# One signal a unit in place of two for TensorE's transposes and products in a graph network's dense stages

## The reference

```
x = layernorm(x + L0(x))   # 2 SAGE convolutions: mean of neighbours @ W_l + b + x @ W_r, rows divided by their norm, relu
x = layernorm(x + L1(x))   # 4 SAGE convolutions without the norm: relu(mean @ W_l + x @ W_r + b)
x = layernorm(x + L2(x))   # attention with 4 heads over the edges, + x @ W1.T + b1, relu, normalised
x = layernorm(x + L3(x))   # transformer convolution over the edges, + x @ Wskip.T + b, relu, batch norm over all nodes
```

## Time and profile before

| what | value |
|---|---|
| median of 3 runs | 16911.43 us (16896.66 to 16914.56) |
| profiled execution | the page gives its span alone: 16848.3 us from the first to the last instruction |
| busy: PE, DVE, ACT, POOL | 8724.5, 7447.1, 4895.5, 7480.4 us |
| mean granted TensorE clock | 0.667 |
| tables of edges, before round 0 | to about 1729 us |
| rounds 0 to 7 end at about | 3350, 5390, 6860, 8340, 9800, 11470, 13860, 16226 us |

### The profile page before, as it was taken

The page is one execution under the profiler, slowest core; times in us unless marked ns, Lnnn a source line. Parts: engine busy times, 40 slices in busy tenths (PEclk is TensorE's granted clock), DMA queues, the critical chain, the costliest instruction groups (busy, mean ns, idle before and its releaser), DMA issues. The chain is left out here.

```text
span 16848.3 us, 221135 instructions
## 1 busy us (share of the span) xinstructions
PE 8724.5 (52%) x38799; PEld 6051.7 (36%) x38898; DVE 7447.1 (44%) x21114; ACT 4895.5 (29%) x11500; POOL 7480.4 (44%) x7460
## 2 busy tenths in 40 slices
PE   6654344533344455445545544454544446677765
PEld 2121233422333344334434433343333323344444
DVE  6654234424454122121112113447888864444456
ACT  0000122223444122122212213344555541222257
POOL 2545554354322654554465455433334336554410
PEclk9775566756666566566656766666666667777776
DMA  6000234424443245345424534554333331233367
GB/s 253 1 3 1 75 120 139 156 71 125 135 143 121 87 148 171 94 126 159 152 88 148 171 97 143 169 190 147 120 121 119 120 113 47 79 98 110 118 193 245
DMA packets 1169327, 2072.17 MB, mean 123 GB/s; under 512 B 283810, under 2 KB 292531, under 8 KB 1156371
## 3 DMA queue, kind: packets, MB, share of 16 engines
q1 hardware_dynamic: 662400, 1128.29, 22.2%
q10 hardware_dynamic: 268534, 564.37, 8.7%
q0 software_dynamic: 238336, 378.92, 8.3%
HBM read 1358.91 MB, written 773.68 MB: 127 GB/s over the span
## 5 line engine op out<-in xcount | busy, mean ns | idle before, releaser
L639 POOL DMA_INDIRECT agg<-y_rows,s_idx x3136 | 3246.2, 1035 | 5507.4 <-ACT y_rows L970 2718.8
L883 PE MATMUL o_bank<-b_parts,ones_parts 3*128 3x512 bf16 (+1 forms) x1568 | 786.2, 501 | 3838.8 <-ACT h_t L1043 2893.0
L886 PE MATMUL o_bank<-w_r,h_t 128*128 128x128 f32 x12544 | 2587.7, 370 | 0.0
L1594 DVE TENSOR_TENSOR total<-o_bank,agg_in 128x512 f32<-128x512 f32 (+1 forms) x1568 | 1048.1, 688 | 3377.2 <-DMA agg_in<-agg 2068.9
L886 PEld LDWEIGHTS o_bank<-w_r,h_t 128*128 128x128 f32 x12544 | 2204.2, 264 | 536.9 <-issue 536.2
L1043 ACT ACTIVATE h_t<-ht_bank 128x512 f32<-128x512 f32 (+1 forms) x1568 | 878.3, 594 | 3930.8 <-remote 2694.1
L883 PEld LDWEIGHTS o_bank<-b_parts,ones_parts 3*128 3x128 bf16 (+1 forms) x1568 | 148.9, 95 | 4192.2 <-ACT h_t L1043 3123.9
L970 ACT ACTIVATE y_rows<-edge_bank,inv 128x128 f32<-128x128 f32 x2352 | 658.7, 373 | 2807.7 <-remote 1640.9
L789 PE MATMUL edge_bank<-w_l,run 128*128 128x128 f32 x4704 | 962.0, 383 | 951.7 <-DVE run L1410 776.4
L630 POOL DMA_INDIRECT gath<-node_a,g_idx x1176 | 1124.9, 957 | 513.6 <-issue 355.1
L630 POOL DMA_INDIRECT gath<-node_x,g_idx x784 | 780.1, 995 | 1079.4 <-PE edge_bank L829 646.1
(11 more groups left out here) (257 smaller groups left out, 14785.5 us busy)
## 6 DMA issues: line engine op xcount, KB each, us to landing
agg_in<-agg SPq DMA_DIRECT2D x1560, 256.0 KB
node_a<-h_out ACTq DMA_DIRECT2D x780, 256.0 KB
h_in<-node_a SPq DMA_DIRECT2D x780, 256.0 KB
node_x<-h_out ACTq DMA_DIRECT2D x392, 256.0 KB
node_b<-h_out ACTq DMA_DIRECT2D x392, 256.0 KB
h_in<-node_x SPq DMA_DIRECT2D x390, 256.0 KB
h_in<-node_b SPq DMA_DIRECT2D x390, 256.0 KB
agg<-zeros ACTq DMA_DIRECT2D x96, 1024.0 KB
```

The source lines that it names most:

```text
L639: pool.indirect_dma_start(agg[order(r)], bass.IndirectOffsetOnAxis(s_idx[q][:, k:k + 1], 0), y_rows[q][:, k, :], None, bounds_check=N - 1, ...
L883: pe.matmul(o_bank[s][0:p, :], ones_parts[:, 0:p], b_parts[:, r, :].unsqueeze(1).to_broadcast([3, RPP, P]), start=True, stop=False, skip_g ...
L886: last = pe.matmul(o_bank[s][0:p, j * P:(j + 1) * P], h_t[s][:, j, 0:p], w_r[r][:], start=False, stop=j == RPP - 1, skip_group_check=True)
L1594: dve.tensor_tensor(flat(total[s], p), o_bank[s][0:p, :], flat(agg_in[s], p), ALU.add).then_inc(sum_ready[s], 1)
```

## The change

`htp_ready` and `mm_ready` become stages with one semaphore for both row groups. PE raises each only after the second group (`if s == 1`), in the eight rounds and in the last stage. All who waited for the semaphore of group s, for either group, now wait for the one semaphore. What is computed and its order on every engine stay.

```
-        htp_ready = unit_stage("htp_ready", all_store)
+        htp_ready = both_stage("htp_ready", all_store)
-        mm_ready = unit_stage("mm_ready", all_store)
+        mm_ready = both_stage("mm_ready", all_store)
...
                     for s in range(2):
-                        sp.wait_ge(htp_ready[s], htp_ready.at(r, u))
+                        sp.wait_ge(htp_ready[0], htp_ready.at(r, u))
                         sp.sem_inc(sp_turn, 1)
                         sp.dma_start(flat(h_in[s], width(u, s)), group_dram(h_of, u, s)).then_inc(h_loaded[s], 16)
...
                             last = pe.transpose(ht_bank[s][:, j * P:j * P + p], h_in[s][0:p, j, :], ident[0:p, 0:p])
-                        last.then_inc(htp_ready[s], 1)
+                        if s == 1:
+                            last.then_inc(htp_ready[0], 1)
...
                                              start=False, stop=j == RPP - 1, skip_group_check=True)
-                        last.then_inc(mm_ready[s], 1)
+                        if s == 1:
+                            last.then_inc(mm_ready[0], 1)
...
-                        act.wait_ge(htp_ready[s], htp_ready.at(r, u + 1))
-                        act.wait_ge(mm_ready[s], mm_ready.at(r, u))
+                        act.wait_ge(htp_ready[0], htp_ready.at(r, u + 1))
+                        act.wait_ge(mm_ready[0], mm_ready.at(r, u))
...
-                        dve.wait_ge(mm_ready[s], mm_ready.at(r, u + 1))
+                        dve.wait_ge(mm_ready[0], mm_ready.at(r, u + 1))
```

## The result

The changed kernel took 16976.29 us (median of 4 runs, 16964.83 to 16999.09) against 16904.04 us (4 runs, 16877.71 to 16914.56) of the kernel before: a ratio of 1.0047, 95% interval 1.0033 to 1.0061. It is **0.5% slower**, where 1.5% faster was forecast. The profiled execution after has a span of 16997.1 us, 148.8 us over that of before, about twice the difference of the medians (72 us), so single stages are to be read with some tens of us of play.

The account below looks back on a forecast made before the run. With no engine busy over 52%, order and waiting were taken to set the time, with PE's signals late during POOL's indirect DMAs. -82 - 83 - 119 - 52 + 75 = -261 us from 16911 gave 16650 us; 8-in-10 range 16350 to 17100.

Parts of the forecast that it names:

- If the signals pass one by one: Sage rounds 2 to 4, POOL's stretches: fewer PE signals let copies come earlier; 19 pairs at 4.3 us, -82 us.
- -119: First sage round: copies and squares move earlier, 5 us for 16 pairs and 3 us for 13 longer ones.
- -52: Sixth sage round: the same gain as in the first, 26 pairs at 2 us each.
- the single signals are delayed as long as four were: Sage rounds, POOL's stretches: the named sign by which the forecast of 16650 us would fail.
- Held in its queue by the reload of h: Longer pairs, rounds 2 to 4: SP's agg load waits behind h's reload; an earlier signal saves 49 x 1.7, 83 us.
- rival B: Signals aren't dear, or the DMAs' end rules; longer pairs keep their length: 16911 within 34 us, or 16950 to 16985; chance 0.20.
- +75 for the coarser signal: Sage rounds outside POOL's stretches: first copy waits for four more transposes, 349 copies at 0.43 us, half taken.
- So I take 0: Transformer round: DVE's sum must clear the same bank before products, hiding the wait; uncovered, 42 or 84 us by clock.
- Attention, 0: Attention round: DVE sets the pace and hides the coarser signal's delay; otherwise 42 us would show.
- Last stage, 0 and at worst +42: Last stage: ACT is the pacer, so the coarser signal costs 0, at worst 42 us.
- Rival A: POOL's stretches: the single signal comes at the later group's hour, so group 0's products move back; 17090 to 17165 us; chance 0.16.
- The prediction's sum by that rule, 16940 us: Whole kernel: at 26.3 ns each, 1764 fewer increments gain at most 46 us, against +75 us for coarser waits.

Follow-up runs that it names:

- before, again: The kernel before, unchanged, profiled again on another chip than that of the first profile: 13983.48 us, ratio 0.9991 to the kernel before.

## Why the prediction was wrong

The sum was -82 - 83 - 119 - 52 + 75 = -261 us; the medians say +72, the profiles +149. All five terms stand for the sage rounds (the other stages were put at 0); these were to get 261 us shorter and took 129 us more.

**"If the signals pass one by one" (-82, and the base of -119 and -52): the step that failed.** It lets the single signal take an earlier place because fewer signals go ahead of it. The profile after has half the signals, on the same chip, and they are as late as before. I counted the units of the sage rounds whose transposes end within 18 us of the pair's first scatter and whose second copy comes over 3 us after them, from the starts and ends of PE's and ACT's instructions. Before there are 199; the first copy comes 10.3 us after its group's transposes, the second 12.9. After there are 197, and either copy comes some 12.5 us after its group's transposes. So the common signal has the lateness of the second group's, and the first group's copy loses 2 us. In the first round 13 units had late copies more than 1.5 us apart before, in the sixth 12: in all 25 the first copy after stands nearer to the place of the second one before than to that of the first, counted from the pair's first scatter.

Pair for pair, counted by the starts of POOL's first scatters, the 19 of rounds 2 to 4 that were to save 82 us are 8 us shorter together. Four became 25.5 us long, the gain that was forecast; four, among them the very pair of the earlier trace rows, grew by 2.4 to 3.0 us, with their copies at 22.3 to 23.1 us, where the second one had been; the others lie between. The 29 pairs of the first round that were to save 119 us are 30 us longer, the 26 of the sixth that were to save 52 are 9 us longer. The signs that were named for the forecast say the same: ACT's unnamed waits rose, POOL's wait for `y_rows` rose, and "the single signals are delayed as long as four were".

That PE's signals are what is late, and not ACT, is right: the trace's semaphore events have `htp_ready[0]` raised at 6111.18 and `htp_ready[1]` at 6116.12, some 12 and 17 us after the transposes of the earlier trace rows. What the lateness counts in is open. It is not the number of these signals alone, as the profile after shows. Nor are PE's signals alone slow: in rounds 2 to 4, over 6 us into a stretch, SP's add instructions that wait for nothing take 0.69 us (median of 120), and in "before, again" never more than 0.04. When the stretch of the earlier trace rows is over, the four signals of PE that are due are all raised within 0.22 us (7971.82 to 7972.04).

**"Held in its queue by the reload of h" (-83): failed.** It was a misreading of the rows before: SP had issued both reloads by 7965.36 (7961.11 + 4.25), 6.4 us ahead of the load of `agg` at 7971.72. In between stand only SP's own small instructions, four of them 0.7 us long. After, both reloads are issued by 8041.5, and the load still comes at 8047.16, some 2.7 us after POOL's last DMA, as before. The 49 longer pairs of rounds 2 to 4 are 13 us longer together and not 83 shorter. That the end of the stretch rules was rival B's reason against the term.

**+75 for the coarser signal: right in kind.** On the chips without late signals it can be seen alone: +98 us in the sage rounds, half by ACT's wait and half by SP's. SP's I had put at 0 ("a load has several us to land").

**"So I take 0" for the transformer round: failed**, +76 us on the first chip, +94 on the others. The cover named there, DVE's sum in the same bank, ended PE's wait in 40 of the 98 units before and in 3 with ACT's wait for both. The bound without cover, 42 us at the high level of the clock and 84 at the low one, holds the first chip's +76, but it counted the wait and not what goes with it in clock: ACT's wait alone cost 107 us, 83 of them in PE's busy time.

**Attention, 0: right** (+7 and 0). DVE is busy for 1977 us of it; that this is why was not tested. **The products' coarser signal** had a part in the +75 (the first sum waits for one more group of products, 1.2 to 2.4 us). On the other chips it cost nothing that shows in any stage; on the first it was not run alone.

**Last stage, 0 and at worst +42: wrong in sign**, -71 us. SP's wait for both groups makes this gain, and ACT's wait for its store goes with it. Why the queue is the quicker for it is not shown.

**The rivals.** Rival A's mark, both copies at the hour of the second, is there in the pair that it was argued from, and in 21 of the 25 units of the first and sixth rounds counted above (within 1 us of the second copy's place in the stretch); in rounds 2 to 4 the single signal comes anywhere between the two hours and beyond. Its price, 181 us or more, was too high: the sage rounds took 129 us more here, and 98 us more on the chips where no signal is late, so what is left for it is some 30 us, within the play of one profile. Rival B's mark, longer pairs that keep their length, is there as well. The time is that of B in its slower form, 16950 to 16985 us, but partly by luck: the sage rounds alone took more than its 75 us, and the transformer round's loss and the last stage's gain, both left out, nearly cancel.

## What to carry to other kernels

Before a wait that is late is counted as gain, follow the pair to its end and ask what else is released at the same hour: here SP's load came with the end of POOL's DMAs whatever PE signalled. Fewer signals are no gain until it is shown that their number is what they wait for. A merged signal delays the first half by the second half's work; in a round that PE paces, four fifths of its price was not the idle time that it added but PE's own work at a lower granted clock (83 of 107 us). Merge signals for each waiter and each stage on its own: the same edit lost 94 us in one stage and gained 67 us in another, by another engine's wait.

## What was not expected of the hardware

The same kernel takes 16904 us on one chip and 13996 to 14008 us on three others. Stages in which POOL issues most take the difference (rounds 2 to 4: 1467 to 1480 us against 1134 to 1137), attention and last stage none (2373 and 2363, 621 and 619). On the slower one ACT's copies follow PE's transposes by 12 and 17 us while POOL issues indirect DMAs; in "before, again" by 0.7 us. Counted as above, 199 units have late copies in the slower chip's profile and 29 to 33 in those of the other chips. On the slower one SP's add instructions are slow as well within the stretches (0.69 us, median, for 0.03). Why isn't known; it may be the chip or something around it.

On a chip without late signals more completion signals cost nothing: 12 more in each of 588 units, between -28 and +11 us in all. The Trainium skill, "TensorE: Matmul & The Clock Gate", section "The cost: per-tile semaphore tail", puts increments at 26.3 ns each, one behind the other; were that on the path, these 7056 would cost 186 us, an estimate from that page's figure. This kernel's runs don't show it, and the first profile's delays of several us are far above it. The prediction's sum by that rule, 16940 us, is within 40 us of the time measured, with the same luck as rival B.

A quarter of a microsecond between two loads went with a large effect: SP's reloads in the last stage, issued in 0.92 in place of 1.16 us, went with 278 in place of 247 GB/s, and the stage is 68 us shorter, of 619.
